# Edge weights copied to PSUM one pair ahead, and the values multiplied by them from there, in a graph layer on one core

## The chip, the cores and the metric

The kernel runs on one core of a Trainium2 chip. The metric is the device time of one execution in microseconds. It is a single launch, with no work on the host between its stages.

## The reference

The reference is one layer over N = 6250 nodes of 512 features and E = 100000 edges sorted by their target: a graph attention, a linear attention over all nodes, and a mixture of experts on the sum. What matters here is the graph attention. With 8 heads of 64 features:

```python
e = el[src] + er[dst];  e = where(e >= 0, e, 0.2 * e)
exp_e = exp(e - segment_max(e, dst)[dst])
a = exp_e / segment_sum(exp_e, dst)[dst]
msg = feat_v[src] * a[:, :, None]
rst = segment_sum(msg, dst)
x = x + rst + attention(xn);  x = x + experts(layernorm(x))
```

The targets are drawn as 6250 u^2, so the first nodes have many more edges than the last.

## The kernel before

Five engines run programs of their own, tied by semaphores. The stages follow one another: normalisation and logits, projections and linear attention (to about 1450 us), the softmax of the edge weights (to about 1580 us), the messages (1580 to about 2900 us), the choice of experts, and the experts. The change lies in the messages.

The 100000 edges are 800 tiles of 125, two tiles to a pair, 400 pairs `u`. The weight of each edge and head (exp_e, not yet divided) lies in SBUF as `EW` [125, 800, 8]. The value rows lie in device memory as `val_tab`, 520 numbers a row: eight heads of 64 and a 1, so that the sum of the weights comes with the sum of the messages. The steps of a tile:

- **GpSimd** (`gather_pair`, L557, the gather itself L559) gathers the 125 rows of a tile into one of the 16 slots of `ring` (8 pairs, in SBUF). It first waits for `tile_free` (L568), which TensorE raises when it has read a slot. With the gather of pair u issued, `report(u - 3)` (L563 to L565) waits until pair u - 3 has landed and raises `vals_ready` by two.
- **VectorE** (`messages`, L1396) waits for `vals_ready` and multiplies the tile in place by its weights, each of the 8 repeated 65 times (L1401), 520 numbers a partition. Both operands are in SBUF.
- **ScalarE** (`onehots`, L1062) makes a matrix of 0 and 1 that says to which of the 125 nodes of the block each edge belongs (L1066, L1069).
- **TensorE** (`block_sums`, `tiles`, L824) multiplies this matrix by the tile, in two halves of 260 columns, summed in PSUM (the helper `mm`, L605). The profile has two matmul records for each half, so four to a tile.

The nodes are 50 blocks of 125. The pairs of block c run from `lo` to `hi`, two numbers that each engine loads from `pairs` (L222) at the start of the block. The pair at the border of two blocks is summed in both; VectorE multiplies it once. After its products of block c VectorE works on finished blocks in the order of `staggered` (L104, L1445): `norm_x1(c-3)` (L1421 to L1423), `make_x1(c-1)` (L1430 to L1441), and last `read_gates(c-5)` (L1411). TensorE's `gates(c-4)` waits for the `gate_read` that L1411 raises (L842), and then it turns a block (L851) and begins the next. Of PSUM's eight banks the stage uses 0 to 3 for the sums, 4 for the turned block and 6 for the gates. Bank 5 is used before the stage, not in it.

In a loop whose counter lives in a register, an instruction whose address depends on the counter is preceded by instructions of the engine's sequencer that work out the address and the value to wait for (FUSED_REGOPS, ALU_OP). The profile shows them as DVEq.

Of the kernel before, what the change touches and what calls it, by code (L numbers as in the profile page):

```python
# [13 lines left out]
H, F = 8, 64  # L14
P = 125
T = N // P
ET = E // P
# [12 lines left out]
ROWS = X * XR  # L30
RING = 16
PAIRS = RING // 2
BEHIND = 3
LAG = 5
NXI = 6
# [3 lines left out]
F1 = F + 1  # L39
DV = H * F1  # L40
# [10 lines left out]
NB = -(-CT // TB)  # L51
# [80 lines left out]
def gps_layer(nc, x, srcT, dstT, dst, W_src, b_src, W_dst, b_dst, W_val, b_val, attn_l, attn_r,  # L132
              Wq, Wk, Wv, Wo, omega_q, omega_k, gate_w, experts, out):
    ctx = ExitStack()
    with ctx:
        def sb(name, shape, dt=FP32):
            return ctx.enter_context(nc.sbuf_tensor(name, shape, dt))

        def sem(name):
            return ctx.enter_context(nc.semaphore(name))  # L140
# [14 lines left out]
        R2 = sb("R2", [128, 16384])  # L155
# [9 lines left out]
        rcnt = sb("rcnt", [P, T])  # L165
        rcnt_ = rcnt[:, :]
        EW = R2[0:P, 0:ET * H].rearrange("p (t h) -> p t h", h=H)
        WS = [R2[:, 6400 + 2048 * i:8448 + 2048 * i].rearrange("p (k n) -> p k n", k=KC) for i in range(4)]
        w_vg, w_k, w_v, w_q = WS
        w_o = WS[0]  # L170

        ring = R2[0:P, 6400:6400 + RING * DV].rearrange("p (s n) -> p s n", s=RING)

        ELP = R2[0:P, 0:ET * H].rearrange("p (g c h) -> p g c h", c=NCH, h=H)

# [37 lines left out]
        kvb = R1[:, 25000:25512].rearrange("p (c n) -> p c n", c=C)  # L213
        kob = R1[:, 25512:26024].rearrange("p (c n) -> p c n", c=C)
        blank = R1[0:P, 25000:25000 + 400]
        accd = R2[0:P, 14720:14720 + T * H].rearrange("p (t h) -> p t h", t=T)
        kvacc = sb("kvacc", [128, 2, 258])

        pairs = sb("pairs", [1, T, 4], INT32)
# [1 line left out]
        def pairs_of(eng_type, c):  # L221
            _, v_ = nc.values_load_multi_w_load_instructions(pairs[0:1, bass.ds(c, 1), 0:2].rearrange("p a n -> p (a n)"), engines=(eng_type,),  # L222
                                                             min_val=0, max_val=ET // 2 - 1)
            return v_
# [73 lines left out]
        iota_b = work[0:P, 4940:4940 + SLOT]  # L298

        ps = ctx.enter_context(nc.psum_tensor("ps", [128, 8, 512], FP32))  # L300

        def two(b, rows=128):
            return ps[0:rows, b:b + 2, 0:500]
# [17 lines left out]
        S = {n: sem(n) for n in names}  # L321
# [5 lines left out]
        xm_out = [sem(f"xm_out{j}") for j in range(2)]  # L327
        gathered = [sem(f"gathered{q}") for q in range(PAIRS)]
        xs_loaded = [sem(f"xs_loaded{q}") for q in range(NX)]
# [148 lines left out]
        def _(eng):  # L478
# [78 lines left out]
            def gather_pair(u):  # L557
                for s in range(2):
                    eng.indirect_dma_start(out=ring[:, (2 * u + s) % RING, :], out_offset=None, in_=val_tab[:, :],  # L559
                                           in_offset=bass.IndirectOffsetOnAxis(ap=src_i[:, 2 * u + s:2 * u + s + 1], axis=0))\  # L560
                        .then_inc(gathered[u % PAIRS], 16)

            def report(u):  # L563
                eng.wait_ge(gathered[u % PAIRS], 32 * (u // PAIRS + 1))
                eng.sem_inc(S["vals_ready"], 2)  # L565

            for u in range(ET // 2):
                eng.wait_ge(S["tile_free"], 2 * u + 2)  # L568
                gather_pair(u)
                if u >= BEHIND:  # L570
                    report(u - BEHIND)
            for u in range(ET // 2 - BEHIND, ET // 2):
                report(u)
# [343 lines left out]
        def _(act):  # L917
# [125 lines left out]

            ew_v = EW.rearrange("p (c g) h -> p g c h", c=NCH)

# [77 lines left out]
        def _(v):  # L1123
# [269 lines left out]

            v.wait_ge(S["weights_kept"], NB)

            def messages(u):  # L1396
                for s in range(2):
                    v.wait_ge(S["vals_ready"], 2 * u + s + 1)
                    r3 = ring[:, bass.ds((2 * u + s) % RING, 1), :].rearrange("p a (h f) -> p (a h) f", h=H)
                    w_ = EW[:, bass.ds(2 * u + s, 1), :].rearrange("p a h -> p (a h)").unsqueeze(2).to_broadcast([P, H, F1])  # L1400
                    v.tensor_tensor(out=r3, in0=r3, in1=w_, op=ALU.mult).then_inc(S["msg_ready"], 1)  # L1401

            def block_messages(c):
                lo, hi = pairs_of(mybir.EngineType.DVE, c)
                with v.If(lo < hi):
                    with v.Fori(lo, hi) as u:
                        messages(u + 1)
# [8 lines left out]
            def x1_row(t, lo, hi):  # L1416
                return acc[:, bass.ds(t, 1), lo:hi].rearrange("p a n -> p (a n)")
# [8 lines left out]
            def make_x1(t):  # L1426
# [13 lines left out]
                st.done(v.bn_aggr(out=mv[0:P, 0, :], in_=st6[0:P, 0, :]))  # L1440
                v.tensor_copy(x1_row(t, D, D + 2), mv[0:P, 0, :]).then_inc(S["var_ready"], 1)  # L1441

            messages(0)

            staggered(v, ((0, block_messages), (3, norm_x1), (1, make_x1), (5, read_gates)), st, 6)  # L1445
# [177 lines left out]
```

## Time and profile before

| | us |
|---|---|
| median of 3 runs | 3313.55 (3311.43 to 3322.34) |
| the profiled execution | 3303.37 |
| its span, first to last instruction | 3301.6 |
| messages, first to last product | 1580 to 2893 |

The profile is of one execution. Its busy times say how long an engine worked, and the idle time before an instruction, with what ended it, says what it waited for. "Issue" is idle time that nothing in the profile explains, such as work of the engine's own sequencer. Times in the timeline count from the start of the span. The mean granted clock of TensorE is 0.898 of full speed over the span.

### The profile page before, as it was taken

The numbers are of one execution on the slowest core, as the hardware profiler recorded it, in microseconds if no ns is written. First come the engines' busy times: TensorE is split into PE (matmuls) and PEld (weight loads), VectorE is DVE, ScalarE is ACT, GpSimd is POOL, SyncE is SP. The second block draws the span as 40 slices with busy tenths as digits, with TensorE's granted clock in tenths as the row PEclk, the third lists the DMA queues.
The fourth block names the chain that finished last, engine by engine and source line by source line (L and its number), as shares of the span: only waits on it lengthen the run. The fifth ranks groups of instructions, "written<-read, shape, count | busy, mean of one in ns | idle before, by whom it ended". The sixth has DMA issues, their size and how long they took to land.

```text
span 3301.6 us, 46378 instructions
## 1 busy us (share of the span) xinstructions
PE 2613.1 (79%) x10455; PEld 1829.8 (55%) x10456; DVE 1554.7 (47%) x2525; ACT 1000.2 (30%) x2564; POOL 2305.7 (70%) x1845
## 2 busy tenths in 40 slices
PE   4659999999999978872666667788888888833998
PEld 2336676677677644431444455666666766732443
DVE  5612222222222268779544444555555566656332
ACT  1312222222222200021444444445556565510111
POOL 7287777777777787776688887888878777700454
PEclk9979999999999998985899998888889898855999
DMA  5331111111111133331465666666776777730111
GB/s 153 128 87 31 32 28 28 36 30 28 30 30 28 24 111 96 99 82 46 122 162 161 168 166 166 182 175 179 187 178 185 185 190 188 182 111 0 38 52 40
DMA packets 276645, 342.22 MB, mean 104 GB/s; under 512 B 164903, under 2 KB 184078, under 8 KB 276468
## 3 DMA queue, kind: packets, MB, share of 16 engines
q0 software_dynamic: 218592, 227.11, 29.8%
q1 hardware_dynamic: 52189, 97.76, 9.1%
q10 hardware_dynamic: 5812, 16.77, 1.5%
q8 instruction: 19, 0.31, 0.0%
q14 instruction: 33, 0.27, 0.0%
HBM read 286.69 MB, written 55.25 MB: 104 GB/s over the span
## 4 chain that ended last, share of the span: by engine, by line
PE 51%; DVE 12%; DMA 11%; issue 10%; POOL 10%; DVEq 1%; ACTq 1%; ACT 1%; SPq 0%; POOLq 0%
PE ps L605 49%; POOL R L559 10%; DMA R<-val_tab,src_i 4%; DMA work<-in_x_dram 4%; DMA xm_tab<-work 2%; DVE work L1291 2%; DMA tb<-tb 1%; DVE work L1491 1%; PE ps L893 1%; DVE R L1401 1%; DVE R L1356 0%; DVE work L1175 0%; DVE R L1389 0%; DVE R L1436 0%; DVE work L1439 0%
## 5 line engine op out<-in xcount | busy, mean ns | idle before, releaser
L605 PE MATMUL ps<-R,work 125*125 (+3 forms) x5240 | 1678.0, 477 | 203.9 <-DVE R L1401 153.7
L605 PEld LDWEIGHTS ps<-R,work 125*125 125x125 f32 (+2 forms) x5240 | 1022.0, 200 | 770.2 <-issue 623.6
L559 POOL DMA_INDIRECT R<-val_tab,src_i x800 | 1053.2, 1316 | 303.2 <-issue 194.8
L522 POOL DMA_INDIRECT R<-el_tab,src_i x800 | 1007.2, 1259 | 337.6 <-issue 337.6
L1401 DVE TENSOR_TENSOR R<-R (+1 forms) x800 | 514.6, 697 | 574.5 <-POOLq L565 418.4
L1069 ACT ACTIVATE work<-work 125x125 f32<-125x125 f32 x900 | 277.7, 309 | 535.7 <-PE ps L605 503.3
L605 PE MATMUL ps<-work,R 128*128 128x250 f32 x1600 | 358.7, 383 | 49.1 <-DVE work L1231 49.1
L1066 ACT ACTIVATE work<-work,negdst 125x125 f32<-125x125 f32 x900 | 353.4, 393 | 112.8 <-issue 88.8
L605 PEld LDWEIGHTS ps<-work,R 128*128 128x128 f32 x1600 | 308.6, 194 | 85.9 <-issue 49.1
L1243 DVE TENSOR_TENSOR R<-ps,R 125x512 f32<-125x512 f32 x50 | 34.6, 692 | 353.7 <-PE ps L605 353.7
L583 POOL DMA_INDIRECT R<-out_dram,work x56 | 55.7, 995 | 202.5 <-DVEq L1564 185.8
L1291 DVE RECIPROCAL work<-ps 128x1000 f32<-128x1000 f32 x25 | 160.1, 6402 | 15.0 <-PE ps L605 14.9
L605 PE MATMUL ps<-R 128*128 (+6 forms) x524 | 128.5, 392 | 27.3 <-DVEq L1560 13.6
L605 PE MATMUL ps<-work 125*128 125x129 f32 (+1 forms) x500 | 80.2, 301 | 81.5 <-issue 74.9
L1118 ACT ACTIVATE work<-ps 128x448 f32<-128x448 f32 x56 | 30.5, 544 | 336.9 <-PE ps L893 336.9
L605 PEld LDWEIGHTS ps<-work 125*128 125x128 f32 (+1 forms) x500 | 61.0, 184 | 115.4 <-issue 115.0
L592 POOL DMA_INDIRECT out_dram<-R,work x56 | 54.1, 966 | 97.4 <-DVE R L1580 97.4
L605 PEld LDWEIGHTS ps<-R 128*128 128x128 f32 (+3 forms) x524 | 81.4, 162 | 72.8 <-issue 32.1
L1580 DVE SCALAR_TENSOR_TENSOR R<-ps,work,R 112x512 f32<-112x512 f32 x56 | 42.0, 751 | 149.5 <-PE ps L605 149.5
L605 PE MATMUL ps<-gw,work 128*125 128x8 f32 x400 | 60.1, 277 | 63.4 <-DVE work L1411 62.8
L1250 DVE TENSOR_SCALAR work<-ps 125x512 f32<-125x512 f32 x50 | 34.6, 692 | 157.1 <-PE ps L605 157.1
L986 ACT ACTIVATE work<-ps 125x512 f32<-125x512 f32 x50 | 29.9, 597 | 246.5 <-PE ps L605 246.5
(250 smaller groups left out, 2153.2 us busy)
## 6 DMA issues: line engine op xcount, KB each, us to landing
work<-in_x_dram SPq DMA_DIRECT2D x50, 500.0 KB
R<-el_tab,src_i POOLq DMA_INDIRECT x800
R<-val_tab,src_i POOLq DMA_INDIRECT x800, 5.8
val_tab<-R SPq DMA_DIRECT2D x50, 253.9 KB
work<-R SPq DMA_DIRECT2D x25, 500.0 KB, 3.6
xm_tab<-work ACTq DMA_DIRECT2D x25, 500.0 KB
work<-xm_tab SPq DMA_DIRECT2D x50, 250.0 KB
out_dram<-R SPq DMA_DIRECT2D x50, 250.0 KB
```

The costliest lines, as they stand in the source:

```text
L522: eng.indirect_dma_start(out=ELP[:, g, c, :], out_offset=None, in_=el_tab[:, :], in_offset=bass.IndirectOffsetOnAxis(ap=src_i[:, t:t + 1], ...
L559: eng.indirect_dma_start(out=ring[:, (2 * u + s) % RING, :], out_offset=None, in_=val_tab[:, :], in_offset=bass.IndirectOffsetOnAxis(ap=sr ...
L583: eng.indirect_dma_start(out=xs[q], out_offset=None, in_=out[:, :], in_offset=bass.IndirectOffsetOnAxis(ap=xs_tok[:, n:n + 1], axis=0), bo ...
L592: eng.indirect_dma_start(out=out[:, :], out_offset=bass.IndirectOffsetOnAxis(ap=xs_tok[:, n:n + 1], axis=0), in_=ys[q], in_offset=None, bo ...
L605: return pe.matmul(o, l, r, start=start, stop=stop)
L1066: fn(absd[s][0:P, :], iota_f[0:P, :], ACT.Abs, bias=negdst[:, bass.ds(2 * u + s, 1)]).then_inc(S["act_step"], 1)
L1069: fn(onehot[s][0:P, :], absd[s][0:P, :], ACT.Relu, scale=-1.0, bias=1.0).then_inc(S["onehot_ready"], 1)
L1243: v.tensor_tensor(out=vout4[:, j, :, 0:F], in0=ps[0:P, 2, :].rearrange("p (h f) -> p h f", h=H), in1=bval.rearrange("p (h f) -> p h f", h= ...
L1250: v.tensor_scalar(phi[0:P, j, :], ps[0:P, 4, :], FCLAMP, None, ALU.min).then_inc(S["fk_read"], 1)
L1291: st.done(v.reciprocal(rq.rearrange("p (b n) -> p b n", b=2), two(2 * b)))
L1401: v.tensor_tensor(out=r3, in0=r3, in1=w_, op=ALU.mult).then_inc(S["msg_ready"], 1)
L1580: v.scalar_tensor_tensor(out=ys[m % NX], in0=ps[0:SLOT, 6 + m % 2, :], scalar=of_slot(2, n), in1=x_, op0=ALU.mult, op1=ALU.add).then_inc(S ...
```

## The change

Bank 5 of PSUM becomes a ring of weights, 32 pairs of 16 numbers. VectorE copies the weights of pair 0 ahead of the loop (`move_weights(0)`). In `messages(u)` it waits for the values of pair u, copies the weights of pair u + 1, waits for the count of `weights_kept` that tells that the copy of pair u (issued one pair earlier) is done, and multiplies both tiles with the weights read from PSUM. `EW` is followed by 16 numbers that nobody uses, for the copy of the pair after the last, so `ring` starts 16 numbers later and `accd` right behind it.

```diff
+WPAIRS = 32
...
+        EW2 = R2[0:P, 0:ET * H + 2 * H].rearrange("p (u h) -> p u h", h=2 * H)
+        RINGLO = ET * H + 2 * H
...
-        ring = R2[0:P, 6400:6400 + RING * DV].rearrange("p (s n) -> p s n", s=RING)
+        ring = R2[0:P, RINGLO:RINGLO + RING * DV].rearrange("p (s n) -> p s n", s=RING)
...
-        accd = R2[0:P, 14720:14720 + T * H].rearrange("p (t h) -> p t h", t=T)
+        accd = R2[0:P, RINGLO + RING * DV:RINGLO + RING * DV + T * H].rearrange("p (t h) -> p t h", t=T)
...
+        weights = ps[0:P, 5, :].rearrange("p (s h) -> p s h", h=H)
+        weights2 = ps[0:P, 5, :].rearrange("p (u h) -> p u h", h=2 * H)
...
+            def move_weights(u):
+                v.tensor_copy(weights2[:, bass.ds(u % WPAIRS, 1), :].rearrange("p a h -> p (a h)"),
+                              EW2[:, bass.ds(u, 1), :].rearrange("p a h -> p (a h)")).then_inc(S["weights_kept"], 1)
+
             def messages(u):
+                v.wait_ge(S["vals_ready"], 2 * u + 1)
+                move_weights(u + 1)
+                v.wait_ge(S["weights_kept"], NB + u + 1)
                 for s in range(2):
                     v.wait_ge(S["vals_ready"], 2 * u + s + 1)
                     r3 = ring[:, bass.ds((2 * u + s) % RING, 1), :].rearrange("p a (h f) -> p (a h) f", h=H)
-                    w_ = EW[:, bass.ds(2 * u + s, 1), :].rearrange("p a h -> p (a h)").unsqueeze(2).to_broadcast([P, H, F1])
+                    w_ = weights[:, bass.ds((2 * u + s) % (2 * WPAIRS), 1), :].rearrange("p a h -> p (a h)").unsqueeze(2).to_broadcast([P, H, F1])
                     v.tensor_tensor(out=r3, in0=r3, in1=w_, op=ALU.mult).then_inc(S["msg_ready"], 1)
...
+            move_weights(0)
             messages(0)
```

## Rows read from the trace of the kernel before

**Rows 1.** The page's part 1, busy time and share of the span by engine

```profile
PE 2613.1 (79%) x10455; PEld 1829.8 (55%) x10456; DVE 1554.7 (47%) x2525; ACT 1000.2 (30%) x2564; POOL 2305.7 (70%) x1845
```

**Rows 2.** The page's part 4, the chain that ended last, shares by line

```profile
PE ps L605 49%; POOL R L559 10%; DMA R<-val_tab,src_i 4%; DMA work<-in_x_dram 4%; DMA xm_tab<-work 2%; DVE work L1291 2%; DMA tb<-tb 1%; DVE work L1491 1%; PE ps L893 1%; DVE R L1401 1%; DVE R L1356 0%; DVE work L1175 0%; DVE R L1389 0%; DVE R L1436 0%; DVE work L1439 0%
```

**Rows 3.** The windows view, halves A, B: length; PE, PEld, DVE, ACT, POOL; clock, DMA, GB/s

```profile
1580.00:2560.00 980.00, 740.39 (x2962) 563.36 (x2963) 484.72 (x862) 474.29 (x1446) 782.64 (x596) 0.90 0.65 171
2560.00:2893.00 333.00, 289.61 (x1252) 233.19 (x1251) 201.99 (x410) 190.82 (x579) 251.11 (x191) 0.88 0.72 185
```

**Rows 4.** The waits view of half A: waiting <- waited for, us, times, longest

```profile
DVE R L1401 <- POOLq L565: 394.5, 206, 5.6
POOL R L559 <- PE ps L605: 67.0, 71, 33.8
```

**Rows 5.** The page's part 5 and the view of line L559

```profile
L559 POOL DMA_INDIRECT R<-val_tab,src_i x800 | 1053.2, 1316 | 303.2 <-issue 194.8
...
L559 POOL DMA_INDIRECT R<-val_tab,src_i x800: 1207/1212/1801, 1526.7 to 2880.5; - x160
DMA to landing us min/median/max: 4.2/5.8/10.9
```

**Rows 6.** The timeline at 1703 us, VectorE and GpSimd

```profile
1703.57 1.31 DVE L1401 TENSOR_TENSOR R<-R  x2 [1.28 <-POOLq L565]
...
1703.68 1.67 POOL L559 DMA_INDIRECT R<-val_tab,src_i  x1 [0.30 <-issue]
1705.65 1.21 POOL L559 DMA_INDIRECT R<-val_tab,src_i  x1 [0.30 <-issue]
```

**Rows 7.** The waits view of half B, and line L222 there

```profile
DVE R L1401 <- issue: 83.7, 22, 5.6
DVE R L1401 <- POOLq L565: 23.9, 16, 3.3
...
L222 DVEq TENSOR_LOAD <-pairs x22: 762/2098/3898, 2559.3 to 2886.6; - x22
```

**Rows 8.** The timeline of late blocks, VectorE, then TensorE

```profile
2788.06 4.97 DVE L1401 TENSOR_TENSOR R<-R  x8 [2.92 <-issue]
...
2797.78 0.17 DVE L1411 TENSOR_SCALAR work<-ps 125x8 f32 x1
2802.03 4.97 DVE L1401 TENSOR_TENSOR R<-R  x8 [4.08 <-issue]
...
2802.58 10.78 PE L605 MATMUL ps<-R,work 125*125 x48 [0.35 <-issue]
2815.87 1.04 PE L605 MATMUL ps<-gw,work 128*125 128x8 f32 x8 [2.51 <-DVE work L1411]
...
2819.67 10.62 PE L605 MATMUL ps<-R,work 125*125 x35
```

**Rows 9.** The timeline of the stage before, VectorE and GpSimd

```profile
1304.39 1.29 DVE L1301 TENSOR_TENSOR work<-work,ps 125x512 f32<-125x512 f32 x2 [2.94 <-DMA work<-in_x_dram]
1304.48 1.21 POOL L522 DMA_INDIRECT R<-el_tab,src_i  x1 [0.31 <-issue]
...
1335.57 1.20 DVE L1294 TENSOR_TENSOR work<-R,work 128x1000 f32<-128x1000 f32 x1 [0.24 <-DVE work L1291]
1336.27 1.58 POOL L522 DMA_INDIRECT R<-el_tab,src_i  x1 [0.30 <-issue]
```

**Rows 10.** The views of lines L1301, L1434 and L1441, ns min/median/max

```profile
L1301 DVE TENSOR_TENSOR work<-work,ps x50: 673/681/689, 1200.0 to 1454.9; 125x512 f32<-125x512 f32 x50
...
L1434 DVE TENSOR_TENSOR R<-R,work x50: 691/693/695, 1831.4 to 2902.0; 125x512 f32 x45, 125x512 f32<-125x512 f32 x5
...
L1441 DVE COPY R<-work x50: 168/169/270, 1834.0 to 2904.6; 125x2 f32 x45, 125x2 f32<-125x2 f32 x5
```

**Rows 11.** VectorE's sequencer in one burst of products, lines L1406 and L1401

```profile
L1406 DVEq FUSED_REGOPS  x4: 74/74/74, 2545.2 to 2548.5; - x4
...
L1401 DVEq FUSED_REGOPS  x12: 53/96/159, 2545.3 to 2548.1; - x12
```

## The prediction

> **What bounds the kernel now.** I read the page's busy shares first: no engine is busy all the time, and the fullest, TensorE with 79%, is followed by GpSimd with 70% [rows 1]. The chain that ended last names TensorE for half of the span and GpSimd's L559 for a tenth [rows 2]. L559 is the gather of the value rows, so the chain runs through the very stretch that the change touches. The change touches nothing outside it but one copy ahead of it, so I cut that stretch, from the first product to the last (1580 to 2893 us), in two and read each half by itself.
>
> In half A (1580 to 2560) GpSimd is busy 783 of 980 us, and in half B (2560 to 2893) 251 of 333 [rows 3]. Nearly all gaps between two gathers are 0.30 us of issue [rows 5, 6], so in A the 596 gathers fill 783 + 596 x 0.30 = 962 of 980 us: **GpSimd sets the pace of A**. The waits say the same from the other side: VectorE's products wait 394.5 us there for GpSimd's report that rows have landed (L565), while GpSimd waits 67 us for TensorE, 33.8 of them in one wait, when the ring fills at the start [rows 4].
>
> Half B is different. It has 22 blocks (one load of `pairs` on VectorE each) in 333 us, so 15.1 us a block [rows 7]. VectorE waits only 23.9 us for GpSimd, in 16 waits, and 83.7 us for its own "issue" [rows 7]. A block of eight products shows what that is: 4.97 us of products, then 4.9 us of work on finished blocks (2793.03 to 2797.95), then 4.08 us until the next product, in which the sequencer loads `pairs` and branches [rows 8]. That is 14 us in which VectorE has nothing to spare: **VectorE and GpSimd share the pace of B**. TensorE is close behind: 48 matmuls (12 tiles) in 10.78 us, then a wait of 2.51 us for VectorE's L1411 [rows 8].
>
> **What the change removes.** A gather takes 1207 ns at least and 1212 in the median, yet 1316 in the mean, and 1801 at most [rows 5]. The surplus is 800 x 0.104 = 83 us. The two timelines show where it comes from: the gather that begins at 1703.68, 0.11 us after a product, takes 1.67 us; the next, at 1705.65 with no product running, takes 1.21 [rows 6]. The 0.46 us more are most of the 0.59 us that the product (0.70 us, the first of the two from 1703.57) still had to run. So a gather that begins while VectorE reads two SBUF operands stands until that instruction is over. The stage before has the control: a gather that begins at 1304.48, inside a product of SBUF by PSUM (L1301), takes 1.21 us, and one at 1336.27, inside one with both operands in SBUF (L1294), takes 1.58 [rows 9]. The changed product is of L1301's kind. I therefore take the surplus away, but for the block work's own instructions with two SBUF operands, which stay: two in each of A's 28 blocks (50 less B's 22), 56 against some 600 products of L1401. I leave 3 us to them.
>
> In A: 596 x (1.313 - 1.212) = 60, less 3 for those, less 9 for the last blocks of A, of some 12 products. TensorE takes the pair at either end of a block twice, so 14 tiles of 10.78/12 = 0.9 us, and from one block's tiles to the next 6.3 us with 2.5 of wait in them [rows 8]: 16.4 us, with 18.2 for GpSimd's twelve. That is near enough, at a granted clock of 0.90 [rows 3], that it can't follow all the way; 1 us in each of nine blocks is my estimate. A gives **-48 us**.
>
> **What a product costs from PSUM.** The row for it is L1301, second operand in PSUM, 512 elements: 681 ns; two SBUF operands of that size take 693 (L1434) [rows 10]. So nothing; the ends are -12 and 0 ns. The Trainium skill (VectorE: DVE Perf Modes, "The TRN2 errata") gives a VectorE instruction a fixed term of 58 cycles from SBUF and 120 from PSUM, at 0.96 GHz; that would be 65 ns on each product, an estimate of 13 us for the 200 of B, which would make the forecast nearly no change. No row here shows such a surcharge.
>
> **What it adds.** For each pair VectorE now (1) waits for the values, (2) computes two addresses and copies 16 numbers of the next pair, (3) waits for the copy of this pair, issued a pair ago and long done, and (4) multiplies twice, each with one address more to wrap. Nothing waits for the copy. What it takes is VectorE's own time, and its sequencer's:
> - Engine: a copy of two numbers takes 169 ns [rows 10]. Products overlap: eight take 4.97 us, so one follows the other by (4.97 - 0.69)/7 = 0.61, some 0.08 less than it lasts [rows 8]. A small copy then costs 0.17 - 0.08 = 0.1 us of a pair. That is the low end.
> - Sequencer: in the burst at 2545 the loop's first instruction comes 4 times from 2545.2 to 2548.5, so 1.1 us a pair, against 2 x 0.61 = 1.22 on the engine [rows 11]. The sequencer has just 0.12 us left. That round is ten instructions: four FUSED_REGOPS and one ALU_OP for the products, FUSED_REGOPS, ALU_OP and COMPARE_BRANCH for the loop, and the two products: 0.11 us each. I count some six more (two FUSED_REGOPS and the copy, an ALU_OP and a wait for `weights_kept`, the wrapping): +0.65, so 1.75 a pair, **0.5 us more than now**. The high end is 0.75, at eight instructions more and none of them fused.
>
> I take 0.5, nearer to the sequencer's rows, because its margin is what the engine's figure leaves out.
>
> In A this is hidden: GpSimd takes 2 x 1.51 = 3.0 us a pair, VectorE needs 1.75. The copy stands behind the wait for the values, so it delays each pair by some 0.4 us, and TensorE behind it (it already waits for L1401 there); the ring of eight pairs covers it. A pair's slot comes free 1.5 (the second gather) + 5.8 (its landing [rows 5]) + 0.5 (VectorE) + 2 (two tiles of TensorE) = 10 us after its first gather starts; with VectorE away for 9 us at a block's end it is 19, and eight pairs less one are 21. If that cover went, GpSimd would wait 1 to 2 us a block.
>
> In B nothing hides it. 100 pairs x 0.5 = +50 us, less what VectorE no longer waits for GpSimd: 191 gathers x 0.10 = 19 us, at most 23.9. So **+31 us**. What is late next is L1411, the last step of VectorE's block, for which TensorE's gate products wait; then GpSimd, which finds its ring full and no longer sets the pace.
>
> Ahead of the loop: one copy, 0.2 us. The moved ring and `accd` keep their sizes: nothing.
>
> **Sum.** -48 + 31 = -17 us. The profiled execution took 3303.4, so 3286; the median of the runs shown is 3313.6, 10 above it, so I give 3297.
>
> **Rivals.**
> 1. *Cheap copies.* If the sequencer's extra work overlaps as the engine's does, a pair costs 0.1 more: B gains -19 + 10 = -9 and A -48: -57, so 3257. For it: the products do overlap. Against: the sequencer has 0.12 us left.
> 2. *Slower: VectorE's sequencer in the last 22 blocks.* At 0.75 us a pair B gains +75 - 19 = +56, and blocks of 12 to 14 products in A lose some of their gain (12 products then take 9 + 6 x 1.97 = 21 us, against 18 of GpSimd), so A gives -38: +18, so 3332. It decides from the point where 100 x p - 19 exceeds 48, p = 0.65 or so. For it: 83.7 us of "issue" in B, and TensorE, kept waiting longer at L1411, may fall to its half clock in more blocks. Against: six instructions would have to cost more than the present ones do.
> 3. *The port stays taken.* If a product with one operand in PSUM still held up a gather, only the cost would be left: B +50, A about 0: 3360. Against it stand the rows of L1301; for it, that L1301 ran beside another gather (el_tab).
> 4. *A dearer operand.* By the surcharge from the Trainium skill named above the forecast becomes about -4; by the trace, an operand from PSUM is no dearer, and I give this little. Worked from rows alone it could come to the 16 ns between the shortest and the longest L1301 [rows 10], 3 us for 200.
>
> **Chances.** Forecast (0.35 to 0.65 a pair, -32 to -2 us) 0.47; rival 1 (-32 to -57) 0.20; rival 2 (-2 to +35) 0.25; rival 3 0.05; rival 4 0.03. About 0.3% (10 us) is what a measurement of this kernel can tell from no change. Faster by more than it: 0.20 + two thirds of 0.47 = 0.52. Slower by more: two thirds of rival 2 and rival 3: 0.22. Within: 0.26. The range leaves out the far end of rival 2 and rival 3 above, and the end of rival 1 below: 3262 to 3336.
>
> **What would show it.** L559's mean should fall from 1316 to below 1225 ns; if it doesn't, rival 3 holds. The 596 gathers of A should be through some 48 us sooner. Eight products in a row in B should take about 4 x 1.75 = 7 us rather than 4.97, and the products' own duration should stay at 690 to 700 ns (about 760 for rival 4). VectorE's waits for L565 should vanish from B, TensorE's for L1411 grow, and GpSimd's for TensorE grow from 24 us. The forecast is wrong if the second half grows by less than 10 or more than 50 us, or if A gains less than 35, say because the ring no longer covers a block's end.

## The result, and the profile after

| | before | after |
|---|---|---|
| median of 4 runs each, on one chip | 3312.49 (3309.49 to 3322.34) | 3281.62 (3279.33 to 3285.71) |
| the profiled execution | 3303.4 | 3281.5 |
| its span | 3301.6 | 3279.7 |
| gather of values, mean ns | 1316 | 1230 |
| first to 600th product (half A) | 974.5 | 933.6 |
| 600th to last product (half B) | 339.3 | 359.6 |
| after the last product | 408.1 | 408.8 |

The changed kernel takes 0.9903 of the time before, interval [0.988, 0.9926]: 31 us less, where 17 were forecast. The medians of the experiments below count every execution; the ratios leave out two that took far longer than all others (3634 us of `e1_late_sbuf_x1_psum`, 9107 us of `e3_x1_in_psum`). The two halves are cut here by the number of products, so that they hold the same work in every kernel (that puts the cut at 2554 us in the kernel before, against 2560 in [rows 3]). Lines 1396 to 1441 of before are 1404 to 1456 now, the gather's L559 is L567 and the matmuls' L605 is L613.

First the two halves in the windows view, here of the kernel before, cut anew (length; busy time and count of PE, PEld, DVE, ACT, POOL; clock, DMA, GB/s):

```profile
1579.69:2554.16 974.47, 736.04 (x2938) 559.84 (x2939) 481.46 (x853) 470.09 (x1434) 778.01 (x592) 0.90 0.65 171
2554.16:2893.44 339.28, 294.41 (x1277) 236.82 (x1276) 205.99 (x421) 195.72 (x594) 255.74 (x195) 0.88 0.72 184
```

The same of the changed kernel:

```profile
1577.64:2511.27 933.63, 725.08 (x2926) 553.33 (x2927) 530.12 (x1153) 468.03 (x1428) 725.02 (x592) 0.90 0.70 179
2511.27:2870.91 359.64, 304.28 (x1291) 243.47 (x1290) 222.68 (x521) 198.22 (x602) 239.19 (x194) 0.86 0.66 174
```

In A the same 592 gathers cost GpSimd 53.0 us less (778.0 to 725.0), and what it idles grew by 12 us: -41. In B GpSimd's busy time fell too, by 16.5 us, and the half still became 20 us longer.

The page's part 5 of the changed kernel, gather, product and copy (busy, mean ns, idle before and its main releaser), answers to [rows 5]:

```profile
L567 POOL DMA_INDIRECT R<-val_tab,src_i x800 | 983.6, 1230 | 349.0 <-issue 180.7
...
L1416 DVE TENSOR_TENSOR R<-R,ps (+1 forms) x800 | 520.9, 693 | 126.9 <-DVE ps L1405 121.6
...
L1405 DVE COPY ps<-R (+1 forms) x401 | 70.0, 175 | 361.3 <-issue 185.7
```

And the view of line L567:

```profile
L567 POOL DMA_INDIRECT R<-val_tab,src_i x800: 1207/1211/1720, 1524.5 to 2854.9; - x160
...
  PE ps L613: 137.8, 109
```

The gather's mean is 1230 ns, 86 less, at the same median. The timeline says why (start, length, idle before): gathers that begin inside a product last 1.21 us, where [rows 6] had 1.67.

```profile
1619.79 1.30 DVE L1416 TENSOR_TENSOR R<-R,ps  x2 [0.44 <-DVE ps L1405]
...
1622.68 0.18 DVE L1405 COPY ps<-R  x1 [1.58 <-POOLq L573]
1623.30 1.30 DVE L1416 TENSOR_TENSOR R<-R,ps  x2 [0.44 <-DVE ps L1405]
...
1619.55 1.21 POOL L567 DMA_INDIRECT R<-val_tab,src_i  x1 [0.30 <-issue]
...
1624.10 1.21 POOL L567 DMA_INDIRECT R<-val_tab,src_i  x1 [0.30 <-issue]
```

The gather at 1624.10 began 0.80 us into the products of 1623.30. Of the 800, I counted 292 that began inside a product; their median is 1211 ns, and two of them last over 1250. In the kernel before, 309 began inside a product, and 252 of them lasted over 1250 ns. What is left of the surplus has another place, a block's end:

```profile
2226.03 1.21 POOL L567 DMA_INDIRECT R<-val_tab,src_i  x1 [0.30 <-issue]
...
2227.42 0.69 DVE L1451 TENSOR_TENSOR R<-work,R  x1 [0.30 <-DVE R L1449]
2227.55 1.64 POOL L567 DMA_INDIRECT R<-val_tab,src_i  x1 [0.30 <-issue]
...
2229.50 1.21 POOL L567 DMA_INDIRECT R<-val_tab,src_i  x1 [0.30 <-issue]
```

L1451, the sum x1, has two SBUF operands. A gather that begins 0.13 us into it lasts 1.64 us. There are 18 gathers over 1.4 us in A, nearly all of them 0.13 to 0.21 us behind the start of an L1451: 18 x 0.43 = 8 us. The kernel before has the same meeting a tenth of a microsecond earlier, and there the gather wins:

```profile
2240.55 0.76 DVE L1436 TENSOR_TENSOR R<-work,R  x1 [0.29 <-DVE R L1434]
2240.58 1.21 POOL L559 DMA_INDIRECT R<-val_tab,src_i  x1 [0.30 <-issue]
```

Begun 0.03 us behind the start of the sum, it lasts its 1.21 us, and the sum 0.76, not 0.69. Of the 41 gathers of before that began inside this instruction, 24 lay 0.02 to 0.05 us behind its start and weren't held at all.

Half B of the changed kernel, the waits view, against [rows 7]:

```profile
DVE ps L1405 <- issue: 83.6, 22, 4.6
POOL R L567 <- PE ps L613: 61.5, 49, 4.3
...
DVE R L1416 <- DVE ps L1405: 24.4, 88, 0.4
PEld ps L613 <- DVE work L1426: 13.6, 13, 2.3
PE ps L613 <- DVE work L1426: 8.1, 11, 1.9
...
DVE R L1416 <- POOLq L573: 3.1, 12, 0.3
```

VectorE hardly waits for GpSimd any more (3.1 us, from 23.9), and GpSimd waits 61.5 us for TensorE (from 24.3, [rows 7] and the same view). VectorE waits for nobody else's work: the time of B goes by VectorE's own round. One of its blocks, against the 4.97 us of products in [rows 8]:

```profile
2786.37 0.18 DVE L1405 COPY ps<-R  x1 [4.62 <-issue]
2786.90 1.30 DVE L1416 TENSOR_TENSOR R<-R,ps  x2 [0.35 <-DVE ps L1405]
2788.12 0.17 DVE L1405 COPY ps<-R  x1
2788.55 1.30 DVE L1416 TENSOR_TENSOR R<-R,ps  x2 [0.26 <-DVE ps L1405]
...
2790.19 1.30 DVE L1416 TENSOR_TENSOR R<-R,ps  x2 [0.25 <-DVE ps L1405]
...
2791.83 1.30 DVE L1416 TENSOR_TENSOR R<-R,ps  x2 [0.25 <-DVE ps L1405]
2793.05 0.15 DVE L1436 RECIPROCAL R<-work  x1
```

A pair takes 1.64 us (2786.90, 2788.55, 2790.19, 2791.83), where it took 1.22. From the first copy to the end of the eighth product it is 6.76 us. The sequencer between 2780 and 2790 us, lines L1405, L1411, L1413 and L1416 (ns min/median/max):

```profile
L1405 DVEq FUSED_REGOPS  x6: 65/110/157, 2786.1 to 2789.6; - x6
...
L1411 DVEq ALU_OP  x3: 40/40/40, 2786.4 to 2789.7; - x3
...
L1413 DVEq EVENT_SEMAPHORE  x3: 21/21/21, 2786.5 to 2789.8; - x3
...
L1416 DVEq FUSED_REGOPS  x9: 76/167/190, 2786.6 to 2789.9; - x9
```

The engine has 0.25 us of idle time ahead of each pair of products: the sequencer, not the copy's 0.17 us, is what a pair costs. Five instructions came with the change: the two FUSED_REGOPS of the copy (L1405), the copy, an ALU_OP (L1411) and the wait (L1413). The last two last 40 and 21 ns. The wrapping of the weights' address added no instruction; it made the products' four FUSED_REGOPS longer, from 383 to 489 ns a pair. I read the sequencer's round, from one branch of the loop to the next, off the two traces: 1.07 us before and 1.64 now.

The same traces split B into the time within the blocks' runs of products and the time between them. Before, 149.6 and 189.7 us; now, 156.9 and 202.8. Of the 100 pairs, 78 follow another pair of the same block, and each of them begins 1.64 us after the one before it, nearly without a wait (1.644 in the mean). The other 22 stand first in a block, and their copy comes between the blocks, 0.53 us ahead of the product.

### The profile page after: what moved, and what is told of

The parts are those of the page before. It is cut to its first block, busy times and chain, and to the rows that moved or that the text cites. A ratio compares the mean times of both kernels' runs of the same rounds, so it can differ in the third digit from the quotient of the medians.

```text
span 3279.7 us, 48375 instructions
## 1 busy us (share of the span) xinstructions
PE 2611.8 (80%) x10455; PEld 1828.9 (56%) x10456; DVE 1620.9 (49%) x2926; ACT 1000.0 (30%) x2564; POOL 2232.7 (68%) x1845
## 4 chain that ended last, share of the span: by engine, by line
PE 46%; DMA 17%; DVE 13%; issue 10%; POOL 9%; DVEq 2%; ACTq 1%; ACT 0%; SPq 0%; POOLq 0%
PE ps L613 44%; POOL R L567 9%; DMA R<-val_tab,src_i 9%; DMA work<-in_x_dram 4%; DMA xm_tab<-work 2%; DVE work L1299 2%; DMA tb<-tb 1%; DVE work L1507 1%; PE ps L901 1%; DVEq L1416 1%; DVE work L1454 0%; DVE R L1451 0%; DVE R L1449 0%; DVE R L1364 0%; DVE work L1183 0%
## 5 line engine op out<-in xcount | busy, mean ns | idle before, releaser
L613 PE MATMUL ps<-R,work 125*125 (+3 forms) x5240 | 1675.5, 477 | 176.0 <-DVE R L1416 120.9
L613 PEld LDWEIGHTS ps<-R,work 125*125 125x125 f32 (+2 forms) x5240 | 1023.4, 200 | 739.2 <-issue 586.3
L567 POOL DMA_INDIRECT R<-val_tab,src_i x800 | 983.6, 1230 | 349.0 <-issue 180.7
L1416 DVE TENSOR_TENSOR R<-R,ps (+1 forms) x800 | 520.9, 693 | 126.9 <-DVE ps L1405 121.6
L613 PE MATMUL ps<-work,R 128*128 128x250 f32 x1600 | 358.5, 383 | 49.8 <-DVE work L1239 49.8
L613 PEld LDWEIGHTS ps<-work,R 128*128 128x128 f32 x1600 | 308.5, 194 | 86.5 <-issue 49.9
L1405 DVE COPY ps<-R (+1 forms) x401 | 70.0, 175 | 361.3 <-issue 185.7
L613 PE MATMUL ps<-work 125*128 125x129 f32 (+1 forms) x500 | 80.0, 301 | 100.9 <-issue 95.1
L613 PE MATMUL ps<-R 128*128 (+6 forms) x524 | 130.5, 396 | 27.4 <-DVEq L1576 13.6
L613 PEld LDWEIGHTS ps<-work 125*128 125x128 f32 (+1 forms) x500 | 61.0, 184 | 134.8 <-issue 134.4
L613 PEld LDWEIGHTS ps<-R 128*128 128x128 f32 (+3 forms) x524 | 81.5, 162 | 74.7 <-issue 35.0
```

The source lines that it names most:

```text
L613: return pe.matmul(o, l, r, start=start, stop=stop)
L1405: v.tensor_copy(weights2[:, bass.ds(u % WPAIRS, 1), :].rearrange("p a h -> p (a h)"), EW2[:, bass.ds(u, 1), :].rearrange("p a h -> p (a h) ...
```

## The experiments

All runs stand beside runs of the kernel before on the same chip, in four sessions on four chips. **Theory 1**: GpSimd paces A and gains the time for which the gathers are no longer held; VectorE's sequencer paces B and loses what the copies cost. **The rival** for B: TensorE paces it and the copies matter little.

**Session 1.** `a0_before` is the kernel before, `a1_after` the changed one.

> The kernel before, once more, with a profile from the same chip as the three runs beside it. The profile on record took 3303.4 us, 9 below its median of 3312.5, while the changed kernel's took 3281.5, which is its median. Theory 1: the 9 us lie between executions of the kernel before. Then this ratio is 1.000 within 0.003, and if this profile takes longer than 3303, the first product to the 600th still takes 974 us and the 200 behind it 339, within 5. Rival: the 9 us belong to the messages, and one of the two halves is then longer by most of them in an execution of 3312.

3302.34 us, 1.0001 [0.9984, 1.0017]; A 975.8, B 341.3 us, both within 5 of the first trace. The profiled execution (3302.5) lay at its median here, so this run doesn't show where the 9 us of a slower one lie.

> The changed kernel on the same chip. Both theories: 0.990, with the first 600 products in 934 us and the last 200 in 360. It is here to be compared with the two behind it.

3328.3 us (3320.7 to 3334.9, 5 runs), 1.008 [1.0053, 1.0108]: the same kernel was slower than before, the opposite of the first measurement. A was 964.5 and B 370.4 us, with the gather's mean at 1229 ns. So the gathers did their part, and something else took 31 us of A and 11 of B. The view of VectorE's loop instructions (L1421) shows where to look. In the trace of the first measurement:

```profile
L1421 DVEq FUSED_REGOPS  x399: 74/74/80, 1579.2 to 2868.7; - x200
L1421 DVEq ALU_OP  x399: 40/40/40, 1581.1 to 2870.1; - x200
```

In `a1_after`:

```profile
L1421 DVEq FUSED_REGOPS  x399: 3/74/718, 1577.2 to 2908.3; - x200
L1421 DVEq ALU_OP  x399: 3/40/712, 1579.0 to 2909.7; - x200
```

An operation on a register that takes 40 ns took up to 712. Over all lines I counted 164 such stops of VectorE's sequencer, 88 us in all (a stop is an instruction that takes over 0.2 us more than the median of its line and operation), and a third of the records of semaphore updates were missing from this trace (27,017, against 40,328); in the first trace there are no stops. All eight traces of sessions 1 and 2 lack a quarter to a third of these records and have stops, `a0_before` too, though just 3 on VectorE; the other ten traces lack none and have no stop. I didn't find what makes the stops, and it isn't shown that they are the whole of the 42 us. `a2_copy_unread` makes the copies and multiplies from SBUF:

```diff
-                    w_ = weights[:, bass.ds((2 * u + s) % (2 * WPAIRS), 1), :]...
+                    w_ = EW[:, bass.ds(2 * u + s, 1), :]...
```

> The copies and their waits as in the changed kernel, but the products read the weights from SBUF. Theory 1 (the gain is the freed port, the price is the sequencer's 0.41 us a pair in the last 200 products): no gain in the first 600 (974 us, or up to 10 more), the last 200 take 339 + 41 less some of the 24 us of waits for GpSimd, so 360 to 375; the whole is 20 to 45 us slower than before, and a gather's mean stays at 1300 to 1320 ns. Rival (the copies shift VectorE in time, and the gathers begin between its products, whatever the operand's place): the first 600 are faster here too, and the whole is about as fast as the changed kernel.

3309.9 us, 1.0018 [0.9996, 1.0039]; A 962.1, B 369.2 us, with 30 stops. The gather's mean was 1278 ns: 38 less than before, by the new rhythm, and 49 more than with the operand from PSUM, so it lies between the two expectations. Gather by gather the answer is plain: 312 began inside a product, and 170 of them lasted over 1250 ns, where `a1_after` has 286 and 2. It is the operand's place that frees a gather inside a product. The time proves nothing, since the two traces were disturbed by different amounts. `a3_no_copies` takes the copies away and keeps the PSUM operand. The weights of the first 32 pairs serve all pairs, so it leaves out the weights of the others:

```diff
-                v.wait_ge(S["vals_ready"], 2 * u + 1)
-                move_weights(u + 1)
-                v.wait_ge(S["weights_kept"], NB + u + 1)
...
-            move_weights(0)
+            v.tensor_copy(ps[0:P, 5, :], R2[0:P, 0:512]).then_inc(S["weights_kept"], 1)
+            v.wait_ge(S["weights_kept"], NB + 1)
```

> The products read PSUM, but the first 32 pairs' weights are copied once ahead of the loop and used again and again; no copy and no extra wait in the loop (it leaves out the weights of the other pairs). Theory 1: the first 600 take 930 us, the last 200 take 339 less the 20 us of shorter gathers, 318 to 328, so the whole is 55 to 62 us below the kernel before; products in a row stand 0.61 us apart. Rival (TensorE bounds the last blocks, the copies cost next to nothing there): the last 200 still take 350 or more and the whole is 25 to 35 us below the kernel before.

3286.93 us, 0.9947 [0.9927, 0.9968]; B 353.0, 17 us less than `a1_after`, but far above the 318 to 328 of theory 1. The profiled execution was its slowest (3316) and has 10 stops. It was repeated in session 3, where the traces are whole.

**Session 2.** 

> The changed kernel once more, to tell which of two results it has. The execution on record has 900 updates of the semaphore onehot_free and no sequencer instruction that takes more than 0.15 us over its usual time; the one of a1_after has 736 and VectorE's sequencer stands still 172 times for up to 0.7 us, 92 us in all. Theory 1 (those stops come from what that chip did while it was profiled, not from the kernel): where there are none, the first 600 products take 934 us, the last 200 take 360, and the ratio is 0.990; where there are, it is above 1.00. Rival (the kernel itself has two ways to run): the ratio is near 1.008 although no sequencer stops.

3278.52 us, 0.9928 [0.9903, 0.9952]. A 947.2 and B 359.1, from a trace with 41 stops (its execution was the slowest of six, 3299). The ratio is below 1 though there are stops, so neither expectation holds as it stands. `b2_block_copies` copies the weights of a whole block at once, at the end of the block before, from block 5 on:

```diff
+            def move_block(c):
+                v.tensor_copy(of_block2[:, bass.ds((c + 1) % 2, 1), :].rearrange("p a n -> p (a n)"),
+                              EW2[:, bass.ds(bounds["hi"] + 1, BPAIRS), :].rearrange("p u h -> p (u h)")).then_inc(S["block_kept"], 1)
```

> From block 5 on the weights of a whole block (26 tiles, 208 numbers) are copied at once, at the end of the block before; the copies and waits of each pair are gone there. It holds for blocks of at most 26 tiles after the fifth, which these edges give. Theory 1 (the price is the sequencer's 0.41 us a pair in the last 200 products): one copy costs 0.4 to 0.7 us a block, 9 to 15 us in the 22 last, so these take 339 + 12 - 20 = 325 to 335 against 360 of the changed kernel, the first 600 as there or 5 us less, and the whole is 25 to 35 us below the changed kernel, 0.980 to 0.984 of the kernel before. Rival (TensorE bounds the last blocks): the last 200 take 350 or more, and the whole is at most 12 us below the changed kernel.

3273.29 us, 0.9914 [0.9889, 0.994]; B 354.7: 5 us below the changed kernel, the rival's numbers. It was no clean test, though: addresses that depend on the pair and the block's first pair cost the sequencer much of what the copy had, and its pair took 1.5 us, not 1.22. `b3_x1_in_psum` keeps the 512 products of the block work in PSUM, so that the sum x1 (L1451) reads one operand there:

```diff
-                st.done(v.tensor_tensor(out=a3, in0=a3, in1=den[0:P, :]..., op=ALU.mult))
+                st.done(v.tensor_tensor(out=prod..., in0=a3, in1=den_..., op=ALU.mult))
...
-                v.tensor_tensor(out=a1, in0=slot_of(t), in1=a1, op=ALU.add)
+                v.tensor_tensor(out=a1, in0=slot_of(t), in1=prod, op=ALU.add)
```

> The changed kernel, with make_x1's two products on the finished block kept in PSUM (den, and the scaled sum in bank 7), so that L1449 and L1451 read one operand from PSUM. In the changed kernel 40 gathers begin while L1451 runs, with two SBUF operands, and take 1.63 us in the median instead of 1.21: 16 us. Theory 1 (the port, by instruction): a gather's mean falls from 1230 to 1213 or so, and the 29 blocks in which GpSimd sets the pace give back 8 to 12 us; the last 200 products don't change. Rival (those stretches lie where GpSimd waits anyway): the mean falls, the time stays within 4 us.

3264.42 us, 0.9883 [0.9857, 0.9909]; gather 1218 ns, A 928.0, B 344.7, where no change of B was expected. `b4_both` has both edits:

> b2_block_copies and b3_x1_in_psum together. Theory 1: the two gains add, 35 to 45 us below the changed kernel, 0.976 to 0.980 of the kernel before, the last 200 products at 320 to 335 us. Rival (TensorE bounds both halves once GpSimd is free): no more than 5 us below the better of the two alone.

3256.14 us, 0.9866 [0.9843, 0.9889]; A 921.9, B 344.3: 22 us below the changed kernel and 8 below b3, which is neither expectation. The gain of b3 in B was not foreseen; session 4 repeats it.

**Session 3.** 

> The changed kernel, beside the three below. Two chips have given 0.990 and 0.993, one 1.008; expected 0.990 to 0.993, the last 200 products in 360 us.

3281.85 us, 0.991 [0.9871, 0.9949]; A 928.7, B 361.7. `d1_no_copies` is `a3_no_copies` again:

> As a3_no_copies (which had stops of the sequencers in it): no copy and no extra wait in the loop, the products from PSUM. Theory 1 (VectorE's sequencer sets the pace of the last 200 products): they take 318 to 330 us, 30 to 40 less than in the changed kernel. Rival (TensorE sets it: in the last blocks it has no gap among a block's tiles, before and after; gates to first tile grew from 3.5 to 4.2 us and the tiles from 11.6 to 11.9): they take 345 to 355, 5 to 15 us less than in the changed kernel, because the products stand 0.61 apart again but TensorE's own round of 15.5 us a block stays.

3263.45 us, 0.9845 [0.9801, 0.9888]. Its windows:

```profile
1583.31:2517.29 933.98, 719.08 (x2925) 548.08 (x2926) 477.76 (x853) 467.34 (x1425) 721.63 (x592) 0.91 0.70 179
2517.29:2855.92 338.63, 295.32 (x1289) 237.87 (x1288) 206.35 (x421) 197.78 (x600) 240.69 (x195) 0.89 0.72 185
```

A is within 5 us of the runs with the copies, so there they are hidden. B is 338.6, below what the rival expected and above theory 1's range: all that the copies cost is back, 23 us against `d0_after`, and **nothing more**. Gathers that are free of the products gain B nothing against the kernel before (339.3), though GpSimd is busy 15 us less. Its waits in B show why:

```profile
DVE R L1413 <- issue: 84.1, 22, 4.8
...
POOL R L567 <- PE ps L613: 39.5, 42, 2.5
...
DVE R L1413 <- POOLq L573: 22.6, 15, 4.1
PEld ps L613 <- DVE work L1423: 12.3, 8, 3.3
PE ps L613 <- DVE work L1423: 9.0, 8, 2.8
```

VectorE waits for GpSimd, GpSimd for TensorE, TensorE for VectorE, each for some 20 to 40 us. I read this as a ring of three, in which one takes as a wait what another saves; no run takes the ring apart. `d2_two_copies` makes each copy twice, the second into a spare bank:

```diff
+                v.tensor_copy(second2[:, bass.ds(u % WPAIRS, 1), :]..., EW2[:, bass.ds(u, 1), :]...).then_inc(S["weights_kept"], 1)
...
-                v.wait_ge(S["weights_kept"], NB + u + 1)
+                v.wait_ge(S["weights_kept"], NB + 2 * u + 2)
```

> Each pair's weights are copied twice, to banks 5 and 7, so that what the copy costs is doubled. One copy more is two FUSED_REGOPS and the copy in the sequencer, 0.3 us a pair. Theory 1: the first 600 products as in the changed kernel within 8 us (GpSimd sets the pace there, a pair then takes VectorE 1.95 of 3.0 us), the last 200 take 30 us more, 390; 1.000 of the kernel before. Rival (TensorE sets the pace of the last 200): they take at most 10 us more than in the changed kernel, as VectorE's 7.8 us for four pairs still lie beside TensorE's 9 us of tiles.

3301.46 us, 0.9968 [0.995, 0.9986]. Its windows:

```profile
1578.98:2518.70 939.72, 727.54 (x2936) 553.91 (x2936) 560.40 (x1453) 469.53 (x1432) 723.34 (x592) 0.90 0.69 178
2518.70:2888.41 369.71, 305.81 (x1281) 242.88 (x1280) 231.10 (x621) 196.60 (x597) 239.44 (x194) 0.86 0.63 169
```

A pair took 1.78 us, 0.145 more, not the 0.3 that was expected. B grew by 8 us against `d0_after` and by 10 against the first trace of the changed kernel. By its number that is the rival's (at most 10 more), but the price was half of what theory 1 took. Split as above, B has 168.2 us within the blocks, 11.3 more than the first trace, and 78 pairs at 0.145 us are 11.3; the time between the blocks hardly moved (201.5). So within the blocks of B VectorE's round passes on its whole cost, as theory 1 has it. A grew by 11 (by 4 against the changed kernel of session 4), which the ring of slots was thought to cover. `d3_late_from_sbuf` multiplies in the last 22 blocks as before the change:

```diff
-            staggered(v, ((0, block_messages),) + rest, st, 6)
+            staggered(v, ((0, block_messages),) + rest, st, 6, ((0, plain_messages),) + rest, 28)
```

> The changed kernel up to block 27, and the last 22 blocks as before the change: no copy, the weights from SBUF. Both theories: the first 600 products as in the changed kernel. Theory 1: the last 200 take 339 as before, so the whole is 20 us below the changed kernel, 0.984 to 0.987 of the kernel before, and GpSimd's stretched gathers return there. Rival (the last 200 are slower for something else than the copies, as the ring's fill at their start): they stay at 350 or more and the whole is within 10 us of the changed kernel.

3265.61 us, 0.9851 [0.9808, 0.9894], A 930.1, B 343.6. The gain of A stays and 18 of the 23 us that B loses to the copies are back: what the change does to one half can be had without the other.

**Session 4.** `e0_after` is the changed kernel, `e3_x1_in_psum` is `b3_x1_in_psum` again, `e2_before_x1_psum` makes that edit on the kernel before, `e1_late_sbuf_x1_psum` joins it to d3.

> The changed kernel, as the measure of the three others. It stood at 0.993 and 0.991 of before in two sessions and at 1.008 in one, whose trace of VectorE's sequencer shows stops that no other trace has in such number. If that session was the odd one, 0.989 to 0.994 here; if the change is in truth worth nothing on some chips, 1.00 or more in some session like this one. In the trace: half A 929 to 936, half B 359 to 362.

3284.43 us, 0.9936 [0.9918, 0.9954]; A 936.2, B 360.1. The changed kernel is faster in four of the five comparisons.

> The changed kernel with the block work's 512 products in PSUM, again, beside the changed kernel in the same session and this time with a trace that may be whole (in its first one, records of semaphores were missing). If what it gave in the first session is the edit's own, the time is 0.995 to 0.997 of the changed kernel here, half B 343 to 348 with 45 to 60 gates-to-tile loads of TensorE and ScalarE at under 1000 ns in the mean; if it came from that session's trace, half B is 358 to 362 and the loads 1300 to 1500 ns.

3267.17 us, 0.9886 [0.9867, 0.9905]. Its windows:

```profile
1576.79:2504.61 927.82, 725.99 (x2939) 555.88 (x2940) 527.32 (x1153) 470.12 (x1435) 717.91 (x593) 0.91 0.70 180
2504.61:2858.22 353.61, 298.77 (x1277) 239.37 (x1276) 221.68 (x521) 196.00 (x595) 234.66 (x194) 0.87 0.67 176
```

And its gather in part 5 of the page:

```profile
L567 POOL DMA_INDIRECT R<-val_tab,src_i x800 | 972.0, 1215 | 347.9 <-issue 177.1
```

17 us less than `e0_after`: A -8.4, which is GpSimd's busy time (724.9 to 717.9) to within 1.4 us, and B -6.5. The 7 us that GpSimd saves are what the stretched gathers behind L1451 were counted at. B fell between the two expectations. `e2_before_x1_psum`:

> The kernel before, with only the block work's 512 products kept in PSUM. In the trace of before the gathers that begin inside the block work's sum (L1436) lasted 44 ns longer each, in that of the changed kernel 40 gathers that began inside the same sum lasted 0.42 us longer. Theory 1 (the time that the sum takes from the gathers comes only with the changed kernel, since in before the products set when a gather can go on): the gather's mean stays at 1300 to 1316, half A 972 to 976, and half B falls by up to 10 us from 339 as the time between the load of pairs and the first tile falls; ratio 0.997 to 1.000. Rival (the sum costs before as much as it costs after): half A falls by 8 us, half B by 14, ratio 0.993.

3299.9 us, 0.9984 [0.9971, 0.9998]. Its windows:

```profile
1582.53:2548.79 966.26, 734.23 (x2944) 557.99 (x2944) 478.98 (x853) 471.18 (x1437) 777.49 (x593) 0.90 0.65 173
2548.79:2883.93 335.14, 287.57 (x1270) 232.10 (x1269) 202.85 (x421) 194.66 (x591) 253.51 (x194) 0.89 0.71 186
```

GpSimd's busy time in A stays (778.0 to 777.5), as theory 1 had it, and yet A is 8 us shorter, in GpSimd's waits, which neither expectation explains (the rival had A's 8 us, but as held gathers, and 14 more in B, which fell by 4); the medians give 7 us for the whole. So the edit is worth some 7 us on the kernel before and 17 on the changed one.

> Two edits on the changed kernel: the last 22 blocks multiply as before the change (values and weights from SBUF, no copies), and the block work keeps its 512 products (between the division and the sum x1) in PSUM. Alone, the first stood at 0.985, the second at 0.988, the changed kernel between 0.991 and 0.993. Theory 1 (VectorE's copies cost half B 20 us, and the block work's two-operand instruction costs half A some 8 us of stretched gathers and every block some 0.7 us between the load of pairs and the first tile, each on its own): the gains add, half A 922 to 930, half B 325 to 335, 3250, ratio 0.981. Rival (both take time from the same slack, and TensorE at some 15.7 us a block is what is left): half B stays at 339 to 345, 3262, ratio 0.985.

3254.02 us, 0.9846 [0.9827, 0.9865], between the two expected times. Its windows:

```profile
1574.55:2500.95 926.40, 723.60 (x2933) 553.82 (x2934) 526.16 (x1153) 469.14 (x1431) 717.90 (x593) 0.91 0.69 180
2500.95:2840.96 340.01, 291.69 (x1279) 234.95 (x1278) 203.47 (x421) 196.30 (x597) 251.43 (x194) 0.89 0.71 184
```

In A x1 in PSUM takes 4 us from what `d3_late_from_sbuf` had (930.1); in B nothing adds: 340.0, the rival's number. It is 53 us faster than the kernel before and 30 faster than the changed one in the same session, so it beats both; `d3_late_from_sbuf` (0.9851) and `b4_both` (0.9866) can't be told from it.

## Why the prediction was right or wrong

**Right.** The mechanism of each half, and both signs: A gained, where GpSimd sets the pace, and B lost, by VectorE's sequencer. The gather's mean was to fall below 1225 and came to 1230, just short. The product's cost from PSUM, put at nothing, was 693 ns (687 to 698), as the two-operand rows of [rows 10]. By the Trainium skill (VectorE: DVE Perf Modes, "The TRN2 errata") it would have been about 760; the trace doesn't show that surcharge. Eight products with their copies took 6.76 us, forecast 7. VectorE's waits for GpSimd all but left B (3.1 us), and GpSimd's for TensorE grew from 24.3 to 61.5. TensorE's for the last step of VectorE's block (L1426, once L1411) were to grow and did not: 13.6 + 8.1 us, against 14.4 + 11.7 in B of the kernel before.

**The size was off**: 17 us forecast and 31 measured. B cost 11 us less than forecast, A gave 7 less, and 9 came with the step from the profile to the median. The terms that failed:
- *"I count some six more"*, and from it "0.5 us more than now" for a pair. It is 1.64 - 1.22 = 0.42. Five instructions came, not six, since the wrapping went into FUSED_REGOPS that were there already. The sequencer's round grew by 0.57 us, not 0.65. So +42 in B, not +50.
- *"less what VectorE no longer waits for GpSimd: 191 gathers x 0.10 = 19 us"*. In the sum it came out (42 - 21 = 21, measured 20.4), but by luck: it is no gain of the freed gathers. `d1_no_copies`, with the same free gathers and no copies, has B at 338.6, against 339.3 before. The wait was cover. The copies filled it, and without them it is there again (22.6 us). Rival 1's gain of 9 us in B doesn't come even where the copies cost nothing.
- *"I leave 3 us to them"*, the block work's own instructions. They took 8 us of A: the gathers that meet the sum x1 now begin 0.13 us behind its start, where most of before began 0.03 us behind it and passed. The rows of before don't show this: the change moves the gathers' starts. GpSimd saved 53 us of A, not 57. *"less 9 for the last blocks of A"*: the idle time grew by 12. A gave -41, not -48.
- *The sum.* These give -41 + 20 = -21, near the profiles' 3303.4 to 3281.5 = -22, and 5 us from the forecast. The other 9 us came with *"the median of the runs shown is 3313.6, 10 above it"*: the profiled execution of before lay 9 us under its median, the profiled one of after at its median. The 10 us were added back as if they belonged to both kernels. In sessions 2 to 4 the medians differ by 24, 31 and 23 us. Whatever makes the slower executions of before, no trace here has one.

**Rival 2** (slower, by VectorE's sequencer in the last 22 blocks) names the true mechanism of B at too high a price: it decides from 0.65 us a pair, and the pair costs 0.42. `a1_after` was slower indeed, with stops of that sequencer that the first trace doesn't have; that they made it slower is not shown. **Rival 3** fell with the gather's mean, and `a2_copy_unread` against `a1_after` (170 of 312 gathers over 1250 ns, and 2 of 286) shows that it is the operand's place. **Rival 4** fell with the products' 693 ns, and **rival 1** with the 0.42 us of a pair.

**Open.** What stops VectorE's sequencer in sessions 1 and 2, and so whether the change gains on every chip. Why x1 in PSUM shortens B by 4 to 15 us, and A of the kernel before by 8. The traces show where the time goes, not why: VectorE's load of `pairs`, in the mean of B's 22 blocks, takes 2.41, 2.45 and 2.41 us in three whole traces of the changed kernel, and 1.84 and 1.72 in `e3_x1_in_psum` and `b3_x1_in_psum`. What sets B at 335 to 344 us where VectorE has time to spare was not taken apart.

## What to carry to other kernels

Read the stage that a change touches in parts with different limits: here one edit gains 41 us where GpSimd paces and loses 20 where VectorE does, and the faster kernel (`d3_late_from_sbuf`, 0.985) uses it in the first part alone. A copy costs what its addresses cost the sequencer (0.42 us a pair, with 0.17 of engine time), and a wait that a cost may fill is cover, not a gain to be booked beside it. Make the sum from profile to profile, and before adding the offset to the median, ask whether it belongs to the kernel or to that one execution.

## What was unexpected of the hardware

- **Stops of a sequencer.** Register operations of 40 to 74 ns take up to 0.72 us, 164 times on VectorE's sequencer in one trace (88 us), 41 times in another and never in three more of the same kernel. They stand in the eight traces from which records of semaphores are missing, 1 to 164 on VectorE and 15 to 47 on SyncE, and in none of the ten whole ones. Stops and missing records go together; which makes the other, or what makes both, isn't shown.
- **Less than 0.05 us decides who is held.** In the kernel before, gathers that begin up to 0.03 us behind the start of a VectorE TENSOR_TENSOR with two SBUF operands are not held (1.21 us), and the instruction lasts up to 0.08 us more. From 0.05 us on they are held; between the two there are some of each. A held gather ends about 1.08 us after the instruction does, so its surplus is the time that the instruction still had to run, less 0.13 us. The starts are regular: 21 of the changed kernel's gathers lie between 0.13 and 0.15 us behind L1451's start, so a stage falls on one side or the other nearly as a whole.
- **A load of two numbers into registers is long and uneven.** It stands ahead of every block of both VectorE and TensorE, 0.5 to 3.3 us. The view of L226 in the changed kernel:

```profile
L226 PEldq TENSOR_LOAD <-pairs x50: 539/1970/2809, 1577.6 to 2863.8; - x50
L226 DVEq TENSOR_LOAD <-pairs x50: 538/2570/3344, 1577.7 to 2862.7; - x50
```
- **TensorE was busy for longer with VectorE's copies.** Its mean granted clock in B was 0.88 before, 0.86 with the copies and 0.89 in `d1_no_copies`, and it was busy 294, 304 and 295 us with the same tiles. From the first gate product to the next block's first tile it took 4.2 us with the copies and 3.5 without, before and in `d1_no_copies`, in the mean of 22 blocks. That the one makes the other is not shown.
